# A hypernet's last rows summed on TensorE instead of moved by DMA, with weights, loads and stores reassigned between engines

## The reference, cut to what matters

```python
dWd = ((h_lang @ Wdd.T + bdd) * DELTA_SCALE).reshape(B, BN, D)
dWu = ((h_lang @ Wdu.T + bdu) * DELTA_SCALE).reshape(B, D, BN)
down = relu(einsum('bld,bnd->bln', x, Wd + dWd) + bd)
x = x + einsum('bln,bdn->bld', down, Wu + dWu) + bu      # L1
h = x * (scale[:, None, :] * rsqrt(ms + EPS))             # L2
u = h @ up_w.T
```

## Time and profile before

| | |
|---|---|
| median of 3 runs | 667.88 us (666.52 to 668.12) |
| the profiled execution | 668.17 us, its span 666.0 us |
| mean granted TensorE clock | 0.973 of full |
| TensorE busy | 617.8 us (93%), 3487 matmuls |
| VectorE busy | 422.9 us (63%) |
| ScalarE busy | 388.4 us (58%) |
| GpSimd (POOL) busy | 92.2 us (14%) |
| read from HBM | 28.32 MB |

### The profile page before, as it was taken

One profiled execution on the slowest core, in us unless ns is written; L12 is line 12 of the kernel. 1 busy time (PEld: TensorE's weight loads), 2 busy tenths in 40 slices (PEclk: granted clock), 3 DMA queues, 4 the chain that ended last, 5 costly groups with the idle time before them and its releaser, 6 DMA issues.

```text
span 666.0 us, 9507 instructions
## 1 busy us (share of the span) xinstructions
PE 617.8 (93%) x3487; PEld 412.1 (62%) x3487; DVE 422.9 (63%) x854; ACT 388.4 (58%) x745; POOL 92.2 (14%) x121
## 2 busy tenths in 40 slices
PE   4777998999999999999999999999999999999797
PEld 2312777644368878744478778544588787454586
DVE  1532796998557574987384766986374757981445
ACT  2400868256884567467875476467854584778610
POOL 1003230122000000820000004510000007400000
PEclk9955999999999999999999999999999999999999
DMA  8998641512000003430000015220000004210000
GB/s 285 386 366 283 201 132 61 120 26 50 2 0 1 2 0 79 90 84 7 0 1 1 0 33 119 57 49 2 1 1 0 1 21 100 69 37 2 0 1 33
DMA packets 34975, 45.08 MB, mean 68 GB/s; under 512 B 4848, under 2 KB 28016, under 8 KB 34800
## 3 DMA queue, kind: packets, MB, share of 16 engines
q1 hardware_dynamic: 30288, 32.30, 17.0%
q0 software_dynamic: 3488, 10.49, 5.8%
q10 hardware_dynamic: 1152, 1.67, 1.2%
HBM read 28.32 MB, written 3.15 MB: 47 GB/s over the span
## 4 chain that ended last, share of the span: by engine, by line
PE 69%; DVE 11%; DMA 9%; ACT 7%; issue 2%; SPq 1%; ACTq 0%
PE psum L1455 22%; PE psum L1732 9%; PE psum L1721 8%; PE psum L1849 8%; PE psum L1677 8%; DVE mx L1284 6%; DMA early_pieces<-in_hyp_w 6%; PE psum L1622 2%; PE psum L1763 2%; DMA arena<-in_hyp_w 2%; PE psum L1567 1%; ACT arena L777 1%; PE psum L1744 1%; ACT act L696 1%; ACT arena L696 1%
## 5 line engine op out<-in xcount | busy, mean ns | idle before, releaser
L922 ACT ACTIVATE arena<-psum 128x512 f32<-128x512 f32 x256 | 140.5, 602 | 56.6 <-PE psum L1721 54.8
L1284 DVE TENSOR_REDUCE mx<-psum 128x1 f32<-128x512 f32 x256 | 159.0, 681 | 19.9 <-PE psum L1677 19.3
L1677 PE MATMUL psum<-kst,qst 96*128 96x512 f32 x192 | 78.9, 438 | 2.7 <-DMA qst<-split 1.0
L1721 PE MATMUL psum<-qst,kst 98*128 98x512 f32 x192 | 77.6, 425 | 3.4 <-ACT arena L922 1.8
L1455 PE MATMUL psum<-upw_hi,kst 128*128 128x512 f32 x256 | 71.3, 400 | 0.4 <-DVE kst L1154 0.4
L1732 PE MATMUL psum<-arena,vals 128*17 128x512 f32 x512 | 67.4, 598 | 1.4 <-ACT arena L922 1.0
L1849 PE MATMUL psum<-act,ghw_hi 128*128 128x512 f32 (+1 forms) x224 | 63.5, 358 | 0.9
L510 POOL DMA_DIRECT2D kst<-split x36 | 18.2, 509 | 321.7 <-DMA kst<-split 281.7
L1677 PEld LDWEIGHTS psum<-kst,qst 96*128 96x128 f32 x192 | 35.8, 188 | 40.5 <-DVE mx L1284 30.3
L1455 PEld LDWEIGHTS psum<-upw_hi,kst 128*128 128x128 f32 x256 | 46.5, 188 | 10.2 <-DVE kst L1154 0.7
L1721 PEld LDWEIGHTS psum<-qst,kst 98*128 98x128 f32 x192 | 35.4, 189 | 23.8 <-ACT arena L922 17.1
(11 more groups left out here) (221 smaller groups left out, 1162.6 us busy)
## 6 DMA issues: line engine op xcount, KB each, us to landing
early_pieces<-in_hyp_w SPq DMA_DIRECT2D x17, 512.0 KB, 8.5
arena<-in_hyp_w SPq DMA_DIRECT2D x15, 512.0 KB, 8.7
kst<-split POOLq DMA_DIRECT2D x36, 128.0 KB, 3.9
qst<-split SPq DMA_DIRECT2D x64, 64.0 KB, 3.7
arena<-in_x SPq DMA_DIRECT2D x4, 512.0 KB, 3.5
arena<-in_up_w POOLq DMA_DIRECT2D x8, 256.0 KB, 4.8
late_pieces<-in_gh_w POOLq DMA_DIRECT2D x8, 256.0 KB, 3.3
out_x<-arena SPq DMA_DIRECT2D x8, 256.0 KB, 2.1
```

The lines of the kernel that those rows point to most:

```text
L922: s.activation(probs[:, kb % 2, i, :], bank[3 + n % RING], ACT.Exp).then_inc(a_p, 1)
L1284: v.reduce_max(mx[:, g % 2, col:col + 1], bank[u % RING], AX.X).then_inc(d_max, 1)
L1677: pe.matmul(bank[u % RING], qst[g % 3][0:KROWS, i, P * t:P * t + P], keys_of(g)[0:KROWS, i // 2, :], start=True, stop=True).then_inc(e_max, 1)
L1721: pe.matmul(bank[3 + k % RING], keys_of(g)[0:SROWS, i // 2, P * kb:P * kb + P], qst[g % 3][0:SROWS, i, :], start=True, stop=True).then_inc ...
```

## The change

- TensorE sums the up weights of batch 0 over the tiles, in place of the 32 moves: `first_rows(n)` multiplies both 256-column halves of tile n of `hy` by 128 columns of a selection matrix `pick`, so that two rows land on partitions of their own, and adds them up in bank 3 over tiles 8 to 15. `first_weights(1)` reads bank 3. POOL builds `pick` at the start (a clear and eight selects).
- `first_rows(n - 1)` stands behind tile n's products from tile 9 on, with five fillers behind it at tiles 11 to 14; `first_rows(15)` and eight fillers stand behind the bottleneck in place of the 26.
- ScalarE does the relus first, then weights 0 to 3, the Sqrt table, weights 4 and 5, then h2. VectorE rounds the last two up weights (6 and 7) itself.
- VectorE does `first_weights(1)` and the bottleneck's low part first, then weights 0 and 1; the other subtractions and its two casts follow h2.
- SP issues the last four stores; POOL clears `qst` ahead of up weights 4 to 7 and waits for the first relu before loading them; the next four loads wait for the sums instead of the stores. The first four stages change places in the arena.

```diff
@@ -222,8 +222,10 @@
-        stage = [cut(col, 512) for col in (3072, 3584, 8192, 8704)]
+        stage = [cut(col, 512) for col in (8192, 8704, 3072, 3584)]
...
+        PICK = 2 * HP - 1
+        pick = late_pieces[:, 0:P + PICK]
@@ -339,15 +340,18 @@
             if h >= 2:
                 eng.wait_ge(hyp_stored[h % 2], 16 * 4 * (h // 2))
-            if n // 4 * 4 - 4 >= HP:
-                eng.wait_ge(hyp_straight[h % 2], 16 * 4 * SLOT * ((n - HP) // 4))
-
-        def move_first(eng, n, r, half):
...
+            if n >= HP + 2 * SLOT:
+                eng.wait_ge(e_rows, n - HP - 2 * SLOT + 1)
@@ -403,13 +401,10 @@
                 if p == 26:
                     fetch_first()
-                if p >= 26 and p % 2 == 0:
-                    move_other_half(p // 2 - 5)
...
-            for n in range(HP + 3, NPIECE):
-                move_other_half(n)
+            store(sp, NPIECE // SLOT - 1)
             fetch_rest()
@@ -497,6 +492,13 @@
+            pool.memset(pick, 0.0).then_inc(pchain, 1)
+            pool.wait_ge(pchain, 3)
+            for g in range(4):
+                for r in range(2):
+                    col = pick[:, PICK + CND * r + 2 * HP * g:PICK + CND * r + 2 * HP * g + 1]
+                    pool.affine_select(out=col, in_=col, compare_op=ALU.not_equal, fill=1.0, base=-(32 * g + 4 * r),
+                                       pattern=[[1, 1]], channel_multiplier=1).then_inc(pchain, 1)
@@ -523,16 +525,20 @@
             pool.wait_ge(e_piece, 2 * NPIECE)
+            for i in range(2):
+                pool.memset(qst[i][:, :, :].bitcast(F32), 0.0).then_inc(queries_zero, 1)
+            pool.wait_ge(a_dn, 1)
+            pool.sem_inc(keys_free, 1)
             for n in range(STAGES, UP):
                 load_stage(n)
-            for i in range(2):
-                pool.memset(qst[i][:, :, :].bitcast(F32), 0.0).then_inc(queries_zero, 1)
+            pool.wait_ge(hyp_moved, 16 * 2)
+            pool.wait_ge(e_rows, HP)
+            pool.sem_inc(keys_free, 1)
+            for n in range(UP, UP + STAGES):
+                load_stage(n)
             for i in range(2):
                 pool.wait_ge(hyp_stored[i], 16 * 4 * NPIECE // SLOT // 2)
...
-            for n in range(UP, NSPLIT):
+            for n in range(UP + STAGES, NSPLIT):
                 load_stage(n)
@@ -968,13 +959,12 @@
-            for k in range(2):
+            front_bottleneck(0, first_dn)
+            for k in range(4):
                 weights(k)
-            front_bottleneck(0, first_dn)
-            for k in range(2, UP):
+            s.activation(warm[:, :], eps6, ACT.Sqrt)
+            for k in range(4, 6):
                 weights(k)
-            store(NPIECE // SLOT - 1)
-            s.activation(warm[:, :], eps6, ACT.Sqrt)
             front_h2(0)
@@ -1125,10 +1115,9 @@
-                step(v.tensor_tensor(hypw[:, 0, cols], hypw[:, 0, cols], base[:, cols], ALU.add))
+                step(v.tensor_tensor(hypw[:, 0, cols], (hypw[:, 0, cols], bank[3][:, 0:D])[m], base[:, cols], ALU.add))
@@ -1396,17 +1385,23 @@
+            first_weights(1)
+            front_bottleneck(0, first_dn)
             for k in range(2):
-                weights(k)
-            front_bottleneck(0, first_dn)
-            first_weights(1)
-            for k in range(2, 4):
                 weights(k)
             front_x2(0, 0, x2T)
             front_x2(0, 1, x2T)
             front_h2(0)
-            for k in range(4, UP):
+            for k in range(2, 4):
                 weights(k)
+            for n in range(UP - 2, UP):
+                v.wait_ge(*staged_in(n))
+                v.tensor_copy(splits[n][1], staged(n)).then_inc(d_qk_hi, 1)
+            for k in range(4, 6):
+                weights(k)
+            for n in range(UP - 2, UP):
+                v.wait_ge(d_qk_hi, n - UP + 3)
+                v.tensor_tensor(splits[n][2], staged(n), splits[n][1], ALU.subtract).then_inc(d_wlo, 1)
             front_rms(0)
@@ -1442,6 +1437,21 @@
+            def first_rows(n):
+
+                pe.wait_ge(*copied(n))
+                for half in range(2):
+                    j = 2 * (n - HP) + half
+                    ins = pe.matmul(bank[3][:, 0:D], pick[:, PICK - j:PICK - j + P],
+                                    hy[:, n // SLOT % 2, n % SLOT, D * half:D * half + D], start=(j == 0),
+                                    stop=(j == 2 * HP - 1))
+                ins.then_inc(e_rows, 1)
...
@@ -1896,6 +1906,12 @@
                 hyp(n)
+                if n == HP:
+                    pe.wait_ge(pchain, 3 + 8)
+                if n > HP:
+                    first_rows(n - 1)
+                if HP + 2 < n < NPIECE - 1:
+                    warm_up(5)
@@ -1906,10 +1922,8 @@
-            for k in range(26):
-                if k == 16:
-                    pe.wait_ge(d_dn, 1)
-                pe.matmul(bank[0], kst[2][:, 0, 0:P], kst[2][:, 0, :], start=True, stop=True)
+            first_rows(NPIECE - 1)
+            warm_up(8)
             front_up(0)
```

More of the change, by code:

```diff
@@ L266, in build @@
         p_rs0 = sem("pool_rs0")
-        hyp_straight = [sem(f"hyp_straight{i}") for i in range(2)]
+        e_rows = sem("pe_first_rows")
         p_alpha_ob, p_wo_alpha = sem("pool_alpha_ob"), sem("pool_wo_alpha")
@@ L329, in build @@
         AT_PARAMS, AT_TURN, AT_WSUM, AT_DOWN = 1, 4, 5, 15
-        MOVED = 16 * 4 * HP // 2
         SMALL = 4
@@ L341, in hyp_free, with store @@
                 eng.wait_ge(hyp_stored[h % 2], 16 * 4 * (h // 2))
-            if n // 4 * 4 - 4 >= HP:
-                eng.wait_ge(hyp_straight[h % 2], 16 * 4 * SLOT * ((n - HP) // 4))
-        def move_first(eng, n, r, half):
[L347 to L350, removed]
+            if n >= HP + 2 * SLOT:
+                eng.wait_ge(e_rows, n - HP - 2 * SLOT + 1)
+        def store(eng, h):
+            m, k = h * SLOT // HP, h * SLOT % HP
+            eng.wait_ge(*copied(SLOT * h + SLOT - 1))
+            for g in range(4):
+                col = (g * HP + k) * 512
+                eng.dma_start(hyp_out[m, :, col:col + SLOT * 512],
+                              hy[32 * g:32 * g + 8, h % 2, :, :].rearrange("p s n -> p (s n)")
+                              ).then_inc(hyp_stored[h % 2], 16)
         block = ctx.enter_context(nc.Block())
@@ L374, in fetch_first @@
                                  ).then_inc(hyp_moved, 16)
[L376 to L380, removed]
             def fetch_rest():
@@ L671, in hyp @@
                                  scale=HYP_SCALE).then_inc(a_hyp, 1)
-                else:
-                    s.wait_ge(d_downq, 1)
-                    s.wait_ge(*copied(n))
-                    for half in range(2):
-                        move_first(s, n, 0, half)
                 if n % SLOT == SLOT - 1 and n < NPIECE - 1:
-                    store(n // SLOT)
+                    store(s, n // SLOT)
             def weights(n):
@@ L1444, in hyp, with warm_up @@
                     ins.then_inc(e_piece, 1)
+            def first_rows(n):
[6 more added lines that the diff above has]
+                ins.then_inc(e_rows, 1)
+            def warm_up(count):
+                for _ in range(count):
+                    pe.matmul(bank[0], kst[2][:, 0, 0:P], kst[2][:, 0, :], start=True, stop=True)
             def product(dst, lhs, rhs, chunks, start=True, stop=True, skip=False, lo_ready=None):
```

18 lines of the change are left out of this document (3 added, 15 removed).

## The result

The changed kernel takes **669.24 us**, the median of 13 runs (666.71 to 670.84), against 667.82 us for 13 runs of the kernel before on the same chip: a ratio of 1.0025, with a 95% interval of 1.0013 to 1.0037. That is about 1.7 us slower (0.0025 x 667.8), where 1.0 us faster was forecast. The profiled execution took 669.24 us with a span of 667.4. The ratios leave out a few disturbed executions, among them the one that was profiled for the first experiment (750.5 us at a mean granted clock of 0.757), of which only the order of events is read.

A forecast was written before the change was run, and what follows sets the result against it. DMA paces the stream from 40 to 62.3 us and VectorE bounds 81 to 102.3. VectorE's first half tile of L2 at 80.1 instead of 81.0, about 1.0 us carried through, gives 666.9 us on the median; range 664.9 to 669.6.

The forecast's parts named there:

- The clock was up: Hypernet stream: unbroken TensorE work from near 43.3 raises the clock by about 48.4, and TensorE then keeps step.
- A tile's sum: TensorE, tiles 8 to 15: 16 products of 256 columns take 1.2 us at full clock, bounds 1.1 and 1.6.
- The last products: End of the last piece's products on TensorE: unchanged at 63.4, bounds 0.9 us earlier and 0.8 later.
- The addend from PSUM: VectorE's addition ahead of the up product: 0.41 us like the SBUF form, at most 0.69.
- The up product: TensorE, behind the bottleneck's subtraction: starts at 69.3, 3.3 us earlier than before, 5 to 6 us behind the last products.
- VectorE's reciprocal: VectorE behind h2: six subtractions, two casts and the reciprocal end last, putting Gelu at 79.4 and its first half tile at 80.1.
- POOL and SP: Loads after the stream: up weights 4 and 5, issued at 67.5 and 68.0, land in 3.4 us; SP's fetch costs nothing.
- The second miss: TensorE's second half tile of L2: last weights at 77.9 and 79.2, done by 80.8, before VectorE asks at 81.6.
- Rival B: ScalarE's h2 slips 1.0 to 3.0 us through late weights 4 and 5, or the clock falls: 667.9 to 669.5, chance 0.22.
- Rival C: TensorE bounds the stream at tiles 9 to 14 if the clock rises late; rise near 57 gives 671; chance 0.12.
- Rival A: Stream ends up to 0.9 us earlier, its last load no longer behind the moves: 666.0, or 665.5; chance 0.20.
- The rule on the shared port: GpSimd's DMA issues beside VectorE's cast block each other: under 0.4 us, giving 667.2 instead of 666.9.

The follow-up runs named there:

- the first experiment: Changed kernel with POOL loading up weights 4 to 7 ahead of the query clears, without waiting for the relu: 667.18 us, ratio 0.9987 to the kernel before.
- e3: Changed kernel with SP waiting for up weights 4 to 7 to land before fetching the rest of the hypernet: 666.32 us, ratio 0.9974 to the kernel before.
- e7: Changed kernel with SP's fetch behind up weights 4 to 7 and ScalarE's h2 ahead of weights 4 and 5: 664.63 us, 0.9952; repeated, 664.52 us, 0.9949.
- e10: The kernel of e7 without the four groups of five fillers in the stream: 663.95 us, ratio 0.9945 to the kernel before.
- e2: Changed kernel with 14 fillers in TensorE's gap between the turn of x2 and the first half tile of L2: 666.92 us, ratio 0.9995.
- e6: The kernel of e3 plus 8 fillers between the turn of x2 and the first half tile: 666.25 us, ratio 0.9974 to the kernel before.
- a0: Changed kernel measured again, unedited: 668.40 us, ratio 1.0014. The ten named there are profiles in which no edit touches what leads up to the up product.
- e4: Changed kernel with up weights 4 to 7 loaded ahead of POOL's clears and 14 fillers in TensorE's gap: 668.65 us, ratio 1.0018 to the kernel before.
- e5: Changed kernel with ScalarE's h2 ahead of up weights 4 and 5, loads as they were: 666.85 us, ratio 0.9988 to the kernel before.
- e8: Changed kernel with the last four stores issued by ScalarE again, behind weights 0 to 3: 668.38 us, ratio 1.0007 to the kernel before.
- e1: Changed kernel with POOL's loads of up weights 4 to 7 ahead of the query clears, no wait for the relu: 667.18 us, ratio 0.9987.
- e9: Changed kernel with ScalarE rounding up weights 6 and 7 as well, ahead of h2, and no casts on VectorE: 671.14 us, ratio 1.0051.

## Why the prediction was wrong, point by point

**What held.** The clock was up at 45.7, by 48.4 in the forecast, so TensorE did not become the bound. A tile's sum took 1.02 to 1.13 us at full clock (forecast 1.2, bounds 1.1 and 1.6). The last products ended at 62.67 (62.06 + 0.61), inside 62.5 to 64.2, and 0.47 of the 0.73 us gained there is the products' own length at full clock (0.61 us, 1.08 before). The addend from PSUM cost 0.42 us (0.41 taken). The up product began 5.3 us behind the last products (5 to 6), at 67.99 where 69.3 was forecast. VectorE's reciprocal was the last thing ahead of Gelu, as forecast, and the VectorE stage kept the shift.

**The step that failed** is in "POOL and SP": "I take 3.4, nearer the low end, because the stream is over by then", and, of the rest of the hypernet, "used much later: no price". Landing took 4.5 and 5.7 us, so ScalarE's h2, which stands behind these loads, came at 73.72 instead of 72.5. The stream was over, but the change itself puts its next transfers there: the prediction noted that the query, key and gate loads no longer wait for the stores and that the fetch goes out behind SP's stores, looked at when their data is used, and gave them no price. Their price is what they take from the loads beside them: e3 put SP's loads off and the landing fell to 3.1 and 3.5 us. It left POOL's query, key and gate loads where they were, so these are not what mattered; SP's were. The 3.4 taken was right for loads without SP's beside them. The busy share of the DMA engines doesn't tell the two cases apart: in 67.4 to 72.6 it is 0.97 in the changed kernel, and 0.91 and 0.99 in e7 and e10, where no load was late. The kernel before had a nearer row than the median 4.4: the same four loads, issued from 63.73 on beside the last moves and stores, took 4.6 to 5.9 us there. With this step out of the way the sign is the forecast one: e3 is 1.7 us faster than the kernel before, where 1.0 was forecast.

**The second miss** is the clock. The forecast had h2 at 72.5; it came 1.2 us late, with the product that feeds it 1.3 us early. So TensorE's gap was 4.38 us, and the clock fell to 1.2 GHz from 73.05 to 79.88. "so it is done by 80.8, before VectorE asks for it at 81.6", of TensorE's second half tile, was worked out at full clock; VectorE's second half tile waited until 83.67. This miss doesn't hang on the late load alone: by the forecast's own times (x2 done at 72.0, 1.09 us of transposes, VectorE's h2 done at 74.7) TensorE would have stood still for about 1.6 us, an estimate, where it had waited 0.45 before; and in e3, with the loads on time, the gap was 2.21 us and the clock fell. The prediction argued from the kernel before that the level held "through a like stretch". The windows of that kernel for the stretch show what it was not like in:

```profile
72.60:81.00 8.40, 7.11 (x34) 5.47 (x34) 5.70 (x11) 8.04 (x18) 2.12 (x4) 1.00 0.69 191
```

TensorE worked 7.11 of 8.40 us there, behind 5.20 of 5.20 in the earlier trace rows that the 26 fillers of the earlier trace rows had filled. In the changed kernel it worked 3.15 of 5.20 and 5.07 of 8.40, the latter partly at half speed.

**Rival B was the case**, both halves of it: its size for a late load, "667.9 to 669.5", holds the 669.24 measured, and the low clock was given "the same size". (666.9 plus the rival's own 3.0 us makes 669.9, not 669.5; nothing hangs on it.) They were offered as two causes for one price. In the runs the late load lengthens the gap and the gap brings the clock down, but each also comes without the other: e3 has the low clock without the late load, e2 the late load without the low clock. Whether the shares found alone (2.7 to 3.4 us for the loads, 1.3 to 2.0 for the clock) add up is open: in e6, removing the second after the first changed nothing in the median, while e7, which has neither, is 4.1 to 5.1 us faster than the changed kernel.

Rival C did not occur: TensorE kept step. Rival A, an earlier end of the stream, is open. In the first profile most of the 0.73 us is the clock's, but in the eleven profiles with the same code up to there (the ten named under a0, and e4) the last products end between 61.69 and 63.04, median 62.5, against 63.40 in the only profile of the kernel before.

**The rule on the shared port** (the Trainium skill, "SBUF — State Buffer") was weighed for DMA issues beside VectorE's cast, at 0.3 us. In the changed kernel the cast beside POOL's DMA issues took 0.29 us, and four issues took 2.12 us, as before: no block to see. The rule's other case, POOL's own SBUF work beside a VectorE copy, showed in e4 (2.36 us).

**Open** are why e6 is no faster than e3, the wide spread of e4 and e5, why the first and second measurement of the changed kernel differ by 0.7 us against the kernel before; how much of the late landing in e8 comes from the stores themselves; whether the two shares add up; and rival A. Loading the query, key and gate weights later wasn't tried.

## What to carry to other kernels

When a change frees queues to issue earlier, price each transfer not by when its data is used but by what is in flight beside it: a load that nobody wants yet can delay the one that an in-order engine stands at. Keep an engine's waits for loads behind the work that another engine is waiting for, and put the unhurried loads behind a wait for the hurried ones. Ahead of a speed-up that shortens a covered stretch, look for what the idle time then left on TensorE does to its clock: work that looked like waste (fillers) may be what kept the next stage at full speed, and once the wait itself is gone it may not be needed.

## What the runs showed of the hardware that was not expected

**A clear on POOL holds back a cast on VectorE.** The same 128x256 cast took 0.29 us behind POOL's two clears, 2.36 us beside them (e4), where it ended 0.15 us behind the second, and 1.60 us in e1. The addition ahead of it, with one operand in PSUM, took 0.42 us beside the clear (e4), no more than the form with both operands in SBUF took without one (0.42). The Trainium skill, "SBUF — State Buffer" (Who interferes with whom), states that a cast can take the port pair that VectorE and GpSimd share, and that the one that comes second waits the whole time; both runs agree with that.

**The clock fell on gaps that look moderate.** With gaps on TensorE of 2.2 us (e3), 3.6 (e8), 3.9 and 4.4 (the changed kernel) and 5.95 (e9), each right behind the 1.09 us of transposes, the clock fell to 0.50 for 3.4 to 6.8 us; with gaps of 0.3 to 0.6 us (e2, e5, e6, e7) it held. In e3 it fell only at 75.45, 1.4 us after work had begun again. No run separates the gap from the light work ahead of it.

**A load is delayed by transfers of another queue, issued after it.** Weights 4 and 5 land in 3.1 and 3.5 us when only POOL's own later loads stand behind them (e3), in 4.5 and 5.7 when SP's fetch is issued 0.2 us after the first of them, and in 3.5 and 4.9 beside stores on ScalarE's queue (e8). With the fetch 1.0 us later (e9) the first two land in 3.2 and 3.6, and the last of the four is late (6.2). The Trainium skill, "DMA: Bandwidth & Descriptors" (Queues, rings and completion order), states that a DMA engine takes turns between the queues that have work for it. The runs agree in kind: what stands behind the load on its own queue left it alone, what came on another did not. No run here shows the turns themselves.

**The Sqrt table load** on ScalarE's path took 1.28 us, and the next activation began 0.02 us behind it (68.52 + 1.28, then 69.82): no further delay is seen. The Trainium skill, "ScalarE: Activation LUTs" (What ACT_TABLE_LOAD costs), gives about 2.66 us for a switch, 1283 ns of load and some 1380 ns of drain; by the trace it is 1.28, without an idle time on either side.
